# Attention and experts block: the four transposes of the next rows moved from behind layer 1 to behind three quarters of it

## The reference

```
xn  = layernorm(x)
out = x + attention(xn) + experts(xn)

attention: 16 heads of 16 features, each token sees the tokens within 64 of it
experts (8 of them, w1 256 x 1024, w2 1024 x 256), best two per token:
  logits = xn @ router_w + router_b ; keep the two largest ; gating = softmax(kept)
  h      = relu(xn @ w1[e] + b1[e])
  y      = h @ w2[e] + b2[e]
  out   += sum over e of gating[e] * y
```

## Time and profile before

| | us |
|---|---|
| median of three runs | 971.83 |
| the runs | 971.32, 971.83, 981.16 |
| profiled execution, its own time | 980.77 |
| span of its trace, first to last instruction | 978.7 |
| TensorE busy in the span | 920.3 (94%) |
| VectorE, ScalarE, GpSimdE busy | 816.5, 739.8, 497.9 |

### The profile page before, as it was taken

The page is one execution under the profiler, slowest core; times in us unless marked ns, Lnnn a source line. Parts: engine busy times, 40 slices in busy tenths (PEclk is TensorE's granted clock), DMA queues, the critical chain, the costliest instruction groups (busy, mean ns, idle before and its releaser), DMA issues. The chain is left out here.

```text
span 978.7 us, 27549 instructions
## 1 busy us (share of the span) xinstructions
PE 920.3 (94%) x7684; PEld 893.4 (91%) x7684; DVE 816.5 (83%) x2170; ACT 739.8 (76%) x1983; POOL 497.9 (51%) x699
## 2 busy tenths in 40 slices
PE   4899799899999999999939999999999999999996
PEld 4788788889999999999829999999999999999996
DVE  5876799988888888888738888888888888888885
ACT  4445799889999999999816777677777666777773
POOL 5210014145555555555534666666666666666663
PEclk9999799999999999999969999999999999999999
DMA  4889324434444444444224212222212222221210
GB/s 152 311 291 308 124 74 119 127 104 149 136 133 135 136 135 136 135 138 130 80 88 112 42 32 41 44 36 36 37 29 42 45 48 43 34 43 34 36 21 1
DMA packets 69868, 95.34 MB, mean 97 GB/s; under 512 B 15550, under 2 KB 48961, under 8 KB 69697
## 3 DMA queue, kind: packets, MB, share of 16 engines
q1 hardware_dynamic: 52800, 77.97, 25.9%
q0 software_dynamic: 17024, 16.88, 10.8%
HBM read 62.91 MB, written 35.53 MB: 101 GB/s over the span
## 5 line engine op out<-in xcount | busy, mean ns | idle before, releaser
L1007 ACT ACTIVATE weights_qkv<-weights_qkv,low 128x256 f32<-128x256 f32 (+1 forms) x512 | 240.2, 480 | 1.3 <-DVE low L818 1.3
L1416 ACT ACTIVATE hid<-ps_experts,b_s 128x256 f32<-128x256 f32 x312 | 130.8, 473 | 133.7 <-PE ps_experts L1482 133.1
L1303 POOL DMA_INDIRECT out<-y,target x78 | 153.6, 1969 | 123.5 <-DVE y L1382 107.2
L829 DVE TENSOR_TENSOR pt<-ps_attend,pt 128x512 fp32r<-128x512 f32 (+1 forms) x256 | 158.4, 620 | 39.2 <-ACT pt L1020 24.9
L1097 PE MATMUL ps_attend<-pt,v_m 128*80 128x256 f32 (+7 forms) x1536 | 187.1, 271 | 2.3 <-DVE inv_t L842 1.6
L1498 PE MATMUL ps_experts<-w_hi,h_hi 128*128 128x256 f32 x624 | 178.6, 286 | 0.8 <-DVE h_lo L1350 0.7
L1482 PE MATMUL ps_experts<-xgt_hi,w_hi 128*128 128x256 f32 x624 | 175.8, 282 | 1.7 <-DVE xgt_lo L1341 1.7
L1498 PE MATMUL ps_experts<-w_hi,h_lo 128*128 128x256 f32 x624 | 175.3, 281 | 0.0
L1498 PE MATMUL ps_experts<-w_lo,h_hi 128*128 128x256 f32 x624 | 175.3, 281 | 0.0
L1482 PE MATMUL ps_experts<-xgt_hi,w_lo 128*128 128x256 f32 x624 | 175.0, 280 | 0.0
L1482 PE MATMUL ps_experts<-xgt_lo,w_hi 128*128 128x256 f32 x624 | 174.9, 280 | 0.0
(11 more groups left out here) (164 smaller groups left out, 2009.2 us busy)
## 6 DMA issues: line engine op xcount, KB each, us to landing
weights_qkv<-in_w SPq DMA_DIRECT2D x15, 1024.0 KB
qk_hi<-weights_qkv SPq DMA_DIRECT2D x16, 512.0 KB, 4.9
qk_lo<-weights_qkv SPq DMA_DIRECT2D x16, 512.0 KB, 5.9
q_st<-qk_hi SPq DMA_DIRECT2D x128, 64.0 KB
k_st<-qk_hi SPq DMA_DIRECT2D x128, 64.0 KB
weights_qkv<-in_x SPq DMA_DIRECT2D x8, 512.0 KB, 4.3
xn_rows<-weights_qkv SPq DMA_DIRECT2D x8, 512.0 KB, 5.1
k_st<-qk_lo SPq DMA_DIRECT2D x64, 64.0 KB
```

The source lines that it names most:

```text
L829: v.tensor_tensor(lo[:, f:l], ps[:, bank_t[h], 0:l - f], hi[:, f:l].bitcast(F32), ALU.subtract).then_inc(s_plo, 1)
L1007: ins = act.activation(wt[:, ring, at_tile(i)], wt[:, ring, at_tile(i)], ACT.Exp, bias=low[:, ring, i:i + 1], scale=-1.0, accum_out=total[ ...
L1303: pool.indirect_dma_start(out_tokens, bass.IndirectOffsetOnAxis(ap=target[:, h:h + 1], axis=0), y[:, h], None, bounds_check=T - 1, oob_is_ ...
L1416: ins = act.activation(hid[:, n % 2, j], ps[:, bank_h[n], j * ROWS:(j + 1) * ROWS], ACT.Relu, bias=b1[:, ds(e * FC + 2 * n + j, 1)])
```

## The change

`transpose_rows` gets a list of chunks, all by default, and does its waits with the first and its signal with the last; as it is called, it still does all four transposes at once. The call for the next step moves from behind layer 1 and the wait for `y` into the loop over the chunks of layer 1, behind chunk 5 of 0 to 7 (`FC` is 8), that is behind 36 of the 48 products. The last step has no call, as before.

```diff
-                def transpose_rows(s, ring):
-                    for h in range(2):
-                        pe.wait_ge(s_g[h], 16 * s + 16)
-                    pe.wait_ge(s_xlo, s + START)
-                    for c in range(DC):
+                def transpose_rows(s, ring, chunks=range(DC)):
+                    if chunks[0] == 0:
+                        for h in range(2):
+                            pe.wait_ge(s_g[h], 16 * s + 16)
+                        pe.wait_ge(s_xlo, s + START)
+                    for c in chunks:
                         for h in range(2):
                             ins = pe.transpose(ps[:, bank_t, (c * 2 + h) * P:(c * 2 + h + 1) * P],
                                                xg[:, ring, h, c * P:(c + 1) * P], g.ident[:])
-                    ins.then_inc(s_tr, 1)
+                    if chunks[-1] == DC - 1:
+                        ins.then_inc(s_tr, 1)
...
                         if m % 2:
                             ins.then_inc(s_l1, 1)
+                        if m == FC - 3 and not final(s):
+                            transpose_rows(s + 1, (turn + 1) % RING)
                     pe.wait_ge(s_y, s + START)
-                    if not final(s):
-                        transpose_rows(s + 1, (turn + 1) % RING)
```

## The result

The changed kernel is faster: 967.37 us median of 14 runs (before 973.75, also 14), ratio 0.9915, 95% interval 0.989 to 0.9941. The forecast was 971.8 us and no change, with a range from 968.8 to 981 us. The times of a kernel fall in groups here, and that has to be known to read them: of 25 executions of the kernel before, run beside the first experiments, 16 lie at 971.4 to 973.7 us and 9 at 979.1 to 981.1; of the 14 of the changed one, 11 lie at 965.5 to 967.8, two at 980.8 and 981.0, and one was disturbed (1508.17).

What follows compares the result with a forecast made beforehand. TensorE's own work was taken to bound the expert stage; moved transposes, seams and covered waits each added 0 us, so the 971.83 us median stayed at 971.8 us, range 968.8 to 981 us.

Steps and rivals of the forecast that it cites:

- What bounds the kernel: Expert stage, 520 to 953 us: TensorE never waits, so only its amount of work or a new wait changes the time.
- The block costs 0.44 us and stays on the path: Four transposes per step on TensorE: 0.44 us each block, 16.8 us over 38 blocks, still on the path after moving.
- The seams, bounds -3 to +3 us: Switches between layer 1, transposes and layer 2: taken as 0 us, at most 0.08 us either way per step.
- Moved work by itself: 0 us: TensorE runs the same transposes 12 products (1.41 us) earlier, nothing added or removed, so the time changes by 0 us.
- The prediction's own sign of being wrong: In the changed profile: PE waiting for the gather or fourth hidden pair, or product starts no longer 0.118 us apart.
- The first rival: Layer 2 products start 0.113 us apart instead of 0.118, winning 8 us: 963.6 us; chance 5%.
- The groups of the times: Runs at 971.32, 971.83 and 981.16 us, profiled one 980.77: difference unreadable from one trace, so the range reaches 981.
- The waits that moved: Waits for gathered rows and the freed transpose bank move into layer 1, between products 36 and 37; both stay covered.
- The fourth pair: Last hidden chunks, from layer 1 through ScalarE and VectorE to layer 2's product 37: 0.44 us later, 1.4 us of cover.
- ScalarE's wait at the start of a step: ScalarE waiting for TensorE absorbs the 0.44 us shift: 2.2 us instead of 2.6.
- The gather's cover: Time between gathered rows landing and their transposes: shrinks from 2.5 to 1.0 us, or 1.9 with the median landing.
- Slower rivals: TensorE waits in layer 2 for late hidden chunks, 988.6 us, 3%; or for the gather, up to 1.41 us a step, 1%.

Runs made afterwards that it cites:

- before_again: The kernel before the change, with no edit, profiled once more: 972.99 us, its steps two slow and two fast in turn, mean period 11.55 us.

## Why the prediction was wrong, point by point

- **What bounds the kernel**: right. No row has TensorE waiting between 520 and 953 us, before and after, and the time moved only by what TensorE spends on its own work.
- **The block costs 0.44 us and stays on the path**: right, 0.44 us in every chain shown.
- **The seams, bounds -3 to +3 us**: the seams themselves are as forecast. This is the step that failed, though: "Moved work by itself: 0 us" priced every product at 0.118 us wherever it stands, and the bounds took in only what a seam costs at the seam. What a seam does to the 48 or 96 products behind it was left out of the sum and put among the rivals. Measured, 84 of 96 products went from 0.1178 to 0.1134 us. The prediction's own sign of being wrong, starts no longer 0.118 us apart, is what came.
- **The first rival**, layer 2 at the shorter pitch: it had the effect, at a chance of 5%, and a size of 8 us, 963.6 us. The measured ratio on the 971.83 us shown is 0.9915 x 971.83 = 963.6 us, but the agreement is luck, from three things that the rival didn't have: layer 1 takes the shorter pitch too (36 of its 48), an execution of the lower group of the kernel before already has part of it (`before_again`), and the ratio leaves out the changed kernel's executions near 981 us. Group against group the gain is 5.3 us. The argument used against it, that layer 1 stays at 0.118 although it follows layer 2 directly, was a misreading: it showed that this seam keeps the pitch that there is (in every profile with all its transposes), not that there is only one. The 28 distances of 0.113 us at the end of the trace stood in the same shapes as the 0.118 ones and had no explanation. That deserved more than 5%.
- **The groups of the times.** The prediction saw 971.3, 971.8, 980.8 and 981.2 us and called the difference unreadable from one trace. It was readable in part: 9 us over 38 steps of 96 products is 0.0025 us a product, and the trace held two pitches 0.0045 apart. It also meant that the profiled execution was the wrong one to sum against.
- **The waits that moved**: right in direction. The fourth pair comes 0.57 us behind layer 1 as before, layer 2 has 1.2 us of cover (1.4 forecast, less 36 x 0.0044 for the faster products), ScalarE's wait at the start of a step is 1.92 us (2.2 forecast). The gather's cover was put at 1.0 us with the longest landing and 1.9 with the median one, both counted from the end of the gather's record, but the profile counts landings from its start. Measured in the changed kernel it is 1.15 us at the least and 2.5 in the median.
- **Slower rivals**: neither wait came up in the changed kernel.

**Shown**: between the profiled executions the gain is a change of pitch and not a wait that is gone; the place of the transposes brings it and the wait for y has no part in it; it doesn't grow with the distance moved; the same program runs in several patterns. **Open**: what makes TensorE take one or the other pitch. Excluded as sole causes are the order of instructions (the kernel before has both), the granted clock (1.00 in all the stretches compared), the operands (the same shapes and lines have both), and the transposes (slow without them). Every product has its own weight load. The load's record starts 2 to 4 ns behind the start of the product before in either pitch, and the product starts 110 ns behind its load where the pitch is fast and 114 to 116 ns where it is slow; the load itself is recorded with 187 to 188 ns in both, in part of the slow ones with 192. So the extra time lies between the start of a load and that of its product; why, no run tells, and none varied the loads. The patterns repeat over one, two or four steps while the loop has three, which speaks for a phase between TensorE's work and something that feeds it; that is argued, not shown.

## What to carry to other kernels

When an engine is busy for 100% of a stretch, count its instructions in that stretch: the busy share can't say whether each takes 113 or 118 ns, and in a stage of 3700 products that is 1.7% of the kernel. Where the same shapes show two distances between starts in one trace, give the difference its full price and a real chance, whatever the edit is meant to do. Where times come in groups, take profiles of more than one group before summing against one; and try a moved block at a few neighbouring places, since one product further may be worth as much as the whole edit.

## What was not expected of the hardware

Products of 128 x 128 by 256 columns at the granted clock of 1.00 (2.4 GHz) start 113.3 or 117.8 ns apart, for dozens to thousands of products in a row, and turn from one to the other within about four products at a seam (from 701.19 to 701.65 us in the changed kernel). The Trainium skill, in TensorE: Matmul & The Clock Gate, section "Wait — 56ns, not 53.3ns?", gives N / 2.4 GHz plus about 2.5 ns between starts of back-to-back products on a warm engine, which for 256 columns is estimated at 109.2 ns. Both measured pitches, here with a weight load for each product, lie above it, by 4.1 and by 8.6 ns. At the lower clock level (1.2 GHz) the kernel before shows only one, 0.213 us between the starts of its first products of layer 1, from 511.1 to 514.3 us. And four useless short products in place of the four transposes made the kernel 12 us slower than the changed one, though the block itself was shorter, 0.40 against 0.44 us.
